# Scan ring of eight units, one C product for two units, two drive products in one instruction, and the state-space norm in the experts' tail

## What is computed

```python
h = _layernorm(x) * (1 + ca) + sa          # state-space norm
u, gate = split(h @ W_in.T)                # 1024 channels each
u = silu(causal_conv(u, 4 taps) + conv_b)
dt, B, C = split(u @ Wx.T); each _rmsnorm
delta = softplus(dt @ Wdt.T + dt_bias)
# scan over tokens t, for each of 1024 channels and 16 states
state = exp(delta_t * A) * state + (delta_t * u_t) * B_t
y_t = sum over states of state * C_t
x = x + ga * ((y + u * D) * silu(gate)) @ W_out.T
```

## Time and profile before

| | us |
|---|---|
| median of 3 runs | 1993.42 (1985.92 to 1998.05) |
| profiled execution, its own time | 1997.48 |
| its span, first to last instruction | 1995.7 |
| start of the state-space stage | 784.65 |
| first scan | 884.79 |
| end of the last scan | 1872.1 |

### The profile page before, as it was taken

How to read it: one execution, slowest core, us unless ns; L and a number is a source line. 1 busy time by engine, 2 the same in 40 slices (tenths; PEclk the granted TensorE clock), 3 DMA queues, 4 the chain that set the end, 5 groups by cost and what they waited for, 6 DMA issues and landing times. The chain is left out here.

```text
span 1995.7 us, 24404 instructions
## 1 busy us (share of the span) xinstructions
PE 1644.5 (82%) x8256; PEld 881.9 (44%) x8256; DVE 1394.3 (70%) x2276; ACT 1083.1 (54%) x1989; POOL 998.4 (50%) x590
## 2 busy tenths in 40 slices
PE   6888999999689994869689697896978969755758
PEld 2522232232256443747356474663746637422422
DVE  3258888886173112048999989899899898999523
ACT  2334666667511112265857668576685766754227
POOL 0000000001054004138898888888888888999413
PEclk8766999999855995869588696896978969766778
DMA  5311000000292436233443444434444344544122
GB/s 220 150 55 50 3 3 3 3 3 4 40 354 98 132 111 231 95 89 92 112 101 85 109 119 108 111 80 106 112 114 117 82 102 106 120 102 98 35 100 85
DMA packets 150747, 191.58 MB, mean 96 GB/s; under 512 B 17715, under 2 KB 122947, under 8 KB 148958
## 3 DMA queue, kind: packets, MB, share of 16 engines
q1 hardware_dynamic: 142508, 167.19, 30.9%
q0 software_dynamic: 4608, 16.80, 2.4%
q10 hardware_dynamic: 3508, 6.05, 0.8%
HBM read 141.81 MB, written 48.18 MB: 95 GB/s over the span
## 5 line engine op out<-in xcount | busy, mean ns | idle before, releaser
L1760 DVE TENSOR_TENSOR_SCAN ssm_scan<-ssm_psum,ssm_state,ssm_scan 128x256 f32<-128x256 f32 x1024 | 678.7, 728 | 49.8 <-ACT ssm_psum L1636 49.3
L1343 POOL TENSOR_TENSOR ssm_scan<-ssm_scan,ssm_bc 128x1024 f32<-128x1024 f32 x256 | 553.5, 2175 | 60.0 <-DVE ssm_scan L1760 58.8
L1636 ACT ACTIVATE ssm_psum<-ssm_rep,ssm_a 128x256 f32<-128x256 f32 x1024 | 433.4, 468 | 168.4 <-DVE ssm_scan L1760 167.9
L1467 PE MATMUL ssm_psum<-ssm_scan,ssm_select 128*32 128x256 f32 x2048 | 204.7, 481 | 199.3 <-POOL ssm_scan L1343 199.2
L1328 POOL TENSOR_TENSOR ssm_scan<-ssm_rep,ssm_bc 128x1024 f32<-128x1024 f32 x128 | 301.1, 2353 | 62.8 <-PE ssm_psum L1467 53.1
L640 ACT ACTIVATE att_probs<-att_psum 128x1024 f32<-128x1024 f32 x256 | 248.3, 1021 | 104.5 <-PE att_psum L576 104.2
L677 DVE TENSOR_REDUCE att_rowmax<-att_psum 128x1 f32<-128x512 f32 x448 | 277.9, 682 | 38.0 <-PE att_psum L558 38.0
L1467 PEld LDWEIGHTS ssm_psum<-ssm_scan,ssm_select 128*32 128x32 f32 x2048 | 45.8, 119 | 316.4 <-POOL ssm_scan L1343 216.4
L529 POOL COPY att_v<-v_tokens 128x128 f32<-128x128 f32 x8 | 2.3, 292 | 328.0 <-ACT att_out L634 328.0
L558 PE MATMUL att_psum<-att_k,att_q 72*128 72x512 bf16 x448 | 159.3, 395 | 3.7 <-DVE att_rowmax L677 2.2
L1745 DVE TENSOR_TENSOR ssm_scan<-ssm_rep,ssm_psum 128x1024 f32<-128x1024 f32 x128 | 155.5, 1215 | 8.5 <-PE ssm_psum L1467 5.8
(11 more groups left out here) (230 smaller groups left out, 1950.9 us busy)
## 6 DMA issues: line engine op xcount, KB each, us to landing
ssm_rep<-drive_rows SPq DMA_DIRECT2D x256, 256.0 KB, 4.4
qkv_wmod<-in_wmod SPq DMA_DIRECT2D x8, 1536.0 KB, 12.2
moe_we<-in_we SPq DMA_DIRECT2D x8, 1024.0 KB, 14.2
ssm_bc<-bc_rows SPq DMA_DIRECT2D x32, 256.0 KB, 4.9
drive_rows<-ssm_delta SPq DMA_DIRECT2D x64, 128.0 KB, 1.7
drive_rows<-ssm_du SPq DMA_DIRECT2D x64, 128.0 KB, 1.8
sorted_rows<-moe_zeros SPq DMA_DIRECT2D x1, 5888.0 KB, 19.1
moe_sorted<-sorted_rows SPq DMA_DIRECT2D x23, 256.0 KB, 3.5
```

Of the source, the lines that this page charges most:

```text
L1343: nc.gpsimd.tensor_tensor(read[:, Q % RING], drive[:, Q % RING], bc[:, c % 2, 1, gr, :].unsqueeze(1).to_broadcast([P, J, SW]), ALU.mult).t ...
L1467: last = nc.tensor.matmul(ps_y[t % 2][32 * j:32 * j + 32, :], select[:], read[:, Q % RING, j, :], start=(gr == 0), stop=False)
L1636: nc.scalar.activation(ps_decay[n % HALF_BANKS][:, i], rep[:, s % 2, 0, j, :], ACT.Exp, scale=amat[:, t, gr, j:j + 1]).then_inc(decay_done, 1)
L1760: nc.vector.tensor_tensor_scan(drive[:, Q % RING, j, :], ps_decay[(2 * Q + j // 2) % HALF_BANKS][:, j % 2], drive[:, Q % RING, j, :], stat ...
```

## The change

In `state_space`:

- the ring has 8 slots;
- GpSimd's drive products of units 0 and 2 of a channel tile are one instruction (`spread(s)`), issued for tile s+1 ahead of the C product of the second unit of tile s; it waits for the copy of tile s+1 in `rep` and for the sum of unit 4s-2;
- the C products of two units are one instruction, after the scans of the second; its semaphore rises by 2 when both are done;
- `drive_input` of tile t+2 stays behind the C product that holds the second unit of tile t;
- the norm of the chunk is gone; chunk data come in normalised, and ScalarE only modulates them, in place, in two buffers;
- the output product adds the residual by two products with the identity, W_out is multiplied with the layer's gate once by GpSimd, and ScalarE copies the result out (`copy_out`); VectorE's `residual` is gone; the gated y overwrites the gate;
- the tables change: "out" goes to units 10, 11, 12, 14, "gate" to 16, 17, 27, 28; ScalarE takes them away at 12, 13, 14, 16 and 18, 19, 29, 30, and the gate's SiLU is at 31;
- of chunk 0, two gate pieces and two step pieces are done in units 0 to 5 (`LATE`) and not ahead of the first scan.

In `experts`: the tail also normalises x (statistics, root, reciprocal, and the product by ScalarE for 12 tiles and by VectorE for 4), stores x with tokens on partitions and the normalised one turned. W_in and W_out lie in the room of the experts' weights, u in that of the turned tiles; half of W_in is loaded in the tail.

```diff
--- before.py
+++ after.py
...
-    RING = 4
+    RING = 8
...
-        AT = {0: ("proj", 0), 1: ("proj", 1), 3: ("conv", 0), 4: ("proj", 2), 5: ("conv", 1), 6: ("proj", 3), 7: ("conv", 2), 8: ("mean", 0),
-              9: ("conv", 3), 10: ("gate", 0), 11: ("gate", 1), 12: ("gate", 2), 13: ("rows", 0), 14: ("gate", 3), 15: ("square", 0),
-              16: ("out", 0), 17: ("out", 1), 18: ("var", 0), 19: ("rms", 0), 20: ("bcast", 0), 21: ("step", 0), 22: ("step", 1),
-              24: ("step", 2), 25: ("step", 3), 27: ("out", 2), 28: ("out", 3)}
-        AHEAD = {"proj": 1, "conv": 1, "gate": 1, "rows": 1, "square": 1, "rms": 1, "step": 1, "mean": 2, "var": 2, "bcast": 2, "out": -1}
-        FIRST = (("mean", 0, 0), ("var", 0, 0), ("bcast", 0, 0), ("proj", 0, 0), ("proj", 0, 1), ("conv", 0, 0), ("proj", 0, 2), ("conv", 0, 1),
-                 ("proj", 0, 3), ("conv", 0, 2), ("conv", 0, 3), ("gate", 0, 0), ("gate", 0, 1), ("rows", 0, 0), ("gate", 0, 2), ("square", 0, 0),
-                 ("gate", 0, 3), ("rms", 0, 0), ("step", 0, 0), ("step", 0, 1), ("step", 0, 2), ("step", 0, 3),
-                 ("mean", 1, 0), ("var", 1, 0), ("bcast", 1, 0))
+        AT = {0: ("proj", 0), 1: ("proj", 1), 3: ("conv", 0), 4: ("proj", 2), 5: ("conv", 1), 6: ("proj", 3), 7: ("conv", 2),
+              9: ("conv", 3), 10: ("out", 0), 11: ("out", 1), 12: ("out", 2), 13: ("rows", 0), 14: ("out", 3), 15: ("square", 0),
+              16: ("gate", 0), 17: ("gate", 1), 19: ("rms", 0), 21: ("step", 0), 22: ("step", 1),
+              24: ("step", 2), 25: ("step", 3), 27: ("gate", 2), 28: ("gate", 3)}
+        AHEAD = {"proj": 1, "conv": 1, "gate": 1, "rows": 1, "square": 1, "rms": 1, "step": 1, "out": -1}
+        FIRST = (("proj", 0, 0), ("proj", 0, 1), ("conv", 0, 0), ("proj", 0, 2), ("conv", 0, 1), ("proj", 0, 3), ("conv", 0, 2), ("conv", 0, 3),
+                 ("rows", 0, 0), ("square", 0, 0), ("rms", 0, 0), ("step", 0, 0), ("gate", 0, 0), ("gate", 0, 1), ("step", 0, 1))
+        LATE = {0: ("gate", 2), 1: ("step", 2), 2: ("gate", 3), 3: ("step", 3)}
...
-        U_COPY, CONV_OUT, GATE_OUT = {3: 0, 4: 1, 7: 2, 9: 3}, {6: 0, 8: 1, 10: 2, 12: 3}, {13: 0, 14: 1, 15: 2, 17: 3}
-        SILU, ROWS_OUT, RMS, SQUARE, GATE_SILU, RSTD, H_OUT = 13, 16, 18, 19, 20, 21, 24
+        U_COPY, CONV_OUT, GATE_OUT = {3: 0, 4: 1, 7: 2, 9: 3}, {6: 0, 8: 1, 10: 2, 12: 3}, {18: 0, 19: 1, 29: 2, 30: 3}
+        SILU, ROWS_OUT, RMS, GATE_SILU, H_OUT = 13, 16, 18, 31, 24
+        LATE_GATE, LATE_STEP, LATE_SILU, LATE_DELTA = {2: 2, 4: 3}, {3: 2, 5: 3}, 5, {3: 2, 5: 3}
         STEP_OUT = {24: 0, 25: 1, 27: 2, 28: 3}
         CARRY_HALO, SAVE_HALO = {1: 0, 2: 1, 6: 2, 8: 3}, {4: 0, 5: 1, 8: 2, 10: 3}
-        CENTRED, NORMED, NORM = 11, 21, 22
+        NORMED = 21
         DELTA = {24: 0, 25: 1, 27: 2, 28: 3}
-        RESIDUAL = {19: 0, 20: 1, 30: 2, 31: 3}
+        OUT_COPY = {12: 0, 13: 1, 14: 2, 16: 3}
...
-            def spread(Q):
-
-                c, q = Q // UNITS, Q % UNITS
-                t, gr = q // GROUPS, q % GROUPS
-                s = c * DT + t
+            def spread(s):
+
+                c, Q = s // DT, s * GROUPS
                 pool.wait_ge(rep_in[s % 2], 64 * (s // 2 + 1))
                 pool.wait_ge(bc_in[c % 2], 64 * (c // 2 + 1))
                 if Q >= RING:
-                    pool.wait_ge(sum_done, Q - RING + 1)
-                    pool.wait_ge(carry_done, (Q - RING) // 2 + 1)
-                nc.gpsimd.tensor_tensor(drive[:, Q % RING], rep[:, s % 2, 1],
-                                        bc[:, c % 2, 0, gr, :].unsqueeze(1).to_broadcast([P, J, SW]), ALU.mult).then_inc(pool_input, 1)
+                    pool.wait_ge(sum_done, Q + 2 - RING + 1)
+                    pool.wait_ge(carry_done, (Q + 2 - RING) // 2 + 1)
+                nc.gpsimd.tensor_tensor(drive[:, Q % RING:Q % RING + 3:2], rep[:, s % 2, 1].unsqueeze(1).to_broadcast([P, 2, J, SW]),
+                                        bc[:, c % 2, 0, 0::2, :].unsqueeze(2).to_broadcast([P, 2, J, SW]), ALU.mult).then_inc(pool_input, 2)
+
+            pool.wait_ge(g.win_in[2], 16)
+            pool.wait_ge(row_out, 1)
+            for t in range(DT):
+                nc.gpsimd.tensor_tensor(wout[:, t], wout[:, t], gate_row, ALU.mult).then_inc(wout_gated, 1)
 
             drive_input(0, 0)
             drive_input(0, 1)
-            for Q in range(2):
-                if not ON_DVE[Q]:
-                    spread(Q)
+            spread(0)
             for c in range(SCH):
                 for q in range(UNITS):
                     t, gr = q // GROUPS, q % GROUPS
                     Q = c * UNITS + q
-                    if Q + 2 < SCH * UNITS and not ON_DVE[(q + 2) % UNITS]:
-                        spread(Q + 2)
-                    pool.wait_ge(scan_done, (Q + 1) * J)
-                    nc.gpsimd.tensor_tensor(read[:, Q % RING], drive[:, Q % RING],
-                                            bc[:, c % 2, 1, gr, :].unsqueeze(1).to_broadcast([P, J, SW]), ALU.mult).then_inc(read_done, 1)
+                    if gr % 2:
+                        if gr == 1 and c * DT + t + 1 < SCH * DT:
+                            spread(c * DT + t + 1)
+                        pool.wait_ge(scan_done, (Q + 1) * J)
+                        pair = slice((Q - 1) % RING, Q % RING + 1)
+                        nc.gpsimd.tensor_tensor(read[:, pair], drive[:, pair],
+                                                bc[:, c % 2, 1, gr - 1:gr + 1, :].unsqueeze(2).to_broadcast([P, 2, J, SW]), ALU.mult).then_inc(read_done, 2)
                     c2, t2 = ahead(c, t)
...
             def output(c, m):
                 if m == 0:
                     pe.wait_ge(ygate_done, (c + 1) * DT)
+                    pe.wait_ge(wout_gated, DT)
                 for t in range(DT):
-                    last = nc.tensor.matmul(bank("out", c, m)[:, 0:SW], wout[:, t, m * P:(m + 1) * P], y[:, c % 2, t, :], start=(t == 0), stop=(t == DT - 1))
+                    nc.tensor.matmul(bank("out", c, m)[:, 0:SW], wout[:, t, m * P:(m + 1) * P], gate[:, c % 2, t, :], start=(t == 0), stop=False)
+                if m == 0:
+                    pe.wait_ge(xres_in, 16 * (c + 1))
+                for s in range(ST):
+                    last = nc.tensor.matmul(bank("out", c, m)[:, s * P:(s + 1) * P], xres[:, s, m * P:(m + 1) * P], g.ident[:], start=False, stop=(s == ST - 1))
...
             def modulate(c):
-                act.wait_ge(norm_done, c + 1)
+                act.wait_ge(x_in[c % 2], 16 * (c // 2 + 1))
                 for k in range(KT):
-                    last = nc.scalar.activation(h[:, k, :], x[:, k, :], ACT.Identity, bias=shift[:, k:k + 1], scale=scale[:, k:k + 1])
+                    last = nc.scalar.activation(h[:, c % 2, k, :], h[:, c % 2, k, :], ACT.Identity, bias=shift[:, k:k + 1], scale=scale[:, k:k + 1])
                 last.then_inc(h_done, 1)
...
+            def copy_out(c, m):
+                act.wait_ge(out_mm, c * KT + m + 1)
+                if m == 0:
+                    act.wait_ge(wout_gated, DT)
+                    if c >= 1:
+                        act.wait_ge(x3_stored, 16 * c)
+                nc.scalar.copy(xout[:, m, :], bank("out", c, m)[:, 0:SW]).then_inc(x3_done, 1)
...
-                if c >= 2:
-                    dve.wait_ge(out_mm, (c - 1) * KT)
-                nc.vector.tensor_tensor(y[:, c % 2, t, :], ps_y[t % 2], gate[:, c % 2, t, :], ALU.mult).then_inc(ygate_done, 1)
-
-            def residual(c, m):
-                if m == 0:
-                    dve.wait_ge(xres_in, 16 * (c + 1))
-                dve.wait_ge(out_mm, c * KT + m + 1)
-                nc.vector.scalar_tensor_tensor(xres[:, m, :], bank("out", c, m)[:, 0:SW], gates[:, m:m + 1], xres[:, m, :],
-                                               ALU.mult, ALU.add).then_inc(x3_done, 1)
...
+            for i in range(SCH):
+                sp.wait_ge(x2_done, (i + 1) * TC)
+                sp.dma_start(xdst[:, i * TC:(i + 1) * TC], x[:, i * TC:(i + 1) * TC]).then_inc(x2_stored, 16)
+                sp.wait_ge(hn_out, (i + 1) * TC)
+                sp.dma_start(hdst[:, :, i * SW:(i + 1) * SW], hnt[:, i % TSLOTS]).then_inc(g.hn_stored[i % TSLOTS], 16)
...
+            act.wait_ge(y_mm, TILES)
+            wsrc = d["win"].rearrange("(k p) m -> p k m", p=P)
+            act.dma_start(win[:, :, 0:DI], wsrc[:, :, 0:DI]).then_inc(g.win_in[0], 16)
...
+            for n in range(TT + 2):
+                if 0 <= n - 2 < TT:
+                    inverse2(n - 2)
+                if n < TT:
+                    add(n)
+                if 0 <= n - 1 < TT:
+                    variance2(n - 1)
+                if 0 <= n - 2 < TT:
+                    normalise2(n - 2)
+                if n < TT:
+                    statistics2(n)
```

320 lines of the change are left out of this document (158 added, 162 removed).

## The result

The changed kernel takes 2362.76 us (median of 4 runs, 2351.13 to 2366.03) against 1994.38 for the kernel before (4 runs, 1985.92 to 1998.05). The ratio is 1.185 with a 95% interval of 1.178 to 1.191: it is slower by over 18%. The forecast was 2292 with a range of 2100 to 2372. The profiled execution took 2366.03, its span is 2364.2.

What follows compares the result with a forecast made beforehand. No engine is full; waits between engines bound the scans, with TensorE without a gap in units 1 to 18. Span 1995.7 + 323 (scans) - 29 (ahead) + 5 (behind) = 2294.7, so 2292 us; range 2100 to 2372.

Steps and rivals of the forecast that it cites:

- the forecast's own run: Whole kernel: 166 a chunk and within some 6 of it, running from 2240 to 2350; chance 0.69.
- the slowest rival: Whole kernel: everything at TensorE's lower clock level and GpSimd products of 4.7, some 2371; chance beyond it 0.05.
- Later sums: TensorE and ScalarE: even units' sums wait for both units' C product, delaying pieces and decays; most of 323 us more.
- The walk: A middle chunk followed unit by unit, each start the latest of its predecessors: 171, or 160 with pieces at 3.65.
- the copy's ring: GpSimd and SyncE: copy 8.4, drive product, C product, delta·u close a ring of 17.7 per tile; alone 2107, chance 0.2.
- 166 for a middle chunk: Scans of chunks 1 to 6: 166 taken for each, with 171 and 160 from the unit-by-unit walk; together 996.
- Chunk 0: First chunk's scans: no output pieces (10 less), late gate and step pieces 14 more; 170.
- The last chunk: Only output pieces: six tiles at 17.7, two at 13.8, 10 for the copies at 12 to 16; 144.
- Two-unit results: ScalarE's output and gate pieces: ahead of an odd unit, two units later costs VectorE 6, three units later 3.3.
- The products: GpSimd's 128x2048 products: C 4.10, drive 4.46, pairing saving at most 48 us; by the skill's figure 38 us more.
- VectorE's lighter chunk: VectorE loses 4.3 per chunk of passes and residuals; not on the path, counted as nothing, 34 us if the bound.
- Ahead of the first scan: Start of the state-space stage: first scan at 855.5 to 856 against 884.79, a gain of 29.

Runs made afterwards that it cites:

- e3: Changed kernel with only delta·u of tile t+2 issued ahead of the drive product and the C product; 2319.8 us, 170.7 per chunk.
- e8: Changed kernel with 14 more filler products on TensorE ahead of the first sum of each channel tile from the second on; 2339.1 us, 171.8 per chunk.
- e10: Changed kernel with both pairings undone, output and gate results taken three units later, gate's SiLU moved behind unit 2's decays; 1944.2 us, 0.977 of the kernel before.
- e2: Changed kernel with only the next tile's drive product issued behind the first pair's C product and delta·u; 2305.6 us, 170.8 per chunk.
- e7: Changed kernel with C and drive products both made for one unit again and the scan ring back at four units; 2037.6 us, 132.8 per chunk.
- e5: Changed kernel with only the tables changed, output and gate pieces taken away three units later instead of two; 2269.3 us, 160.5 per chunk.

## Why the prediction was right, and where its steps were off

The side and the mechanism held: the pairs make TensorE's sums late, its pieces with them, and ScalarE and VectorE wait for the pieces in their queues. The size held less well. 2292 is 71 too low, and 2362.76 lies above the forecast's own run of 2240 to 2350. It is inside the stated range only because that was stretched to the slowest rival, 2371, which counted products of 4.7 where 4.16 was measured; that part is luck. Of the signs named in advance, GpSimd's waits for the copy (131), the scans' waits for decays (327), the C product (4.16) and the clock (0.77) came as said; the chunk (174.8, not 160 to 171) and the first scan (863.3, not 856) did not.

- **Later sums.** The walk can be laid beside the trace, tile by tile (means of chunks 1 to 6, from first scan to first scan):

| channel tile | 1 | 2 | 3 | 4 | 5 | 6 | 7 | 8 | chunk |
|---|---|---|---|---|---|---|---|---|---|
| walk, lower clock behind idle time | 18.5 | 18.1 | 24.7 | 26.1 | 21.6 | 20.7 | 18.8 | 22.5 | 171 |
| changed kernel | 19.5 | 20.9 | 24.7 | 26.5 | 21.3 | 21.0 | 19.2 | 21.6 | 174.8 |
| e3, delta·u first | 19.5 | 16.7 | 24.9 | 26.0 | 21.6 | 21.0 | 18.5 | 22.4 | 170.7 |

All but the second are within 1.0. The second is 2.8 too short in the walk, and e3 says why: it opens the copy's ring alone, and the second tile falls by 4.2. The wait for the copy in the timeline above (4.94 ahead of the drive product at 1415.54) is one of these. A wait that I had not counted also shows there: VectorE's carry of the halo, the tokens that the convolution needs from before (L1760), waits 34.5 us for the convolution in six waits of chunks 1 to 6, 7.69 in the timeline above. ScalarE waits for the same piece, and the scans behind it wait 0.30 more for their decays, so by itself it costs little.
- **166 for a middle chunk is the step that failed in size.** Measured were 174.8; the six chunks together took 1048.5 and not 996, which is 52.5 of the 71. Of the 8.8 per chunk, 5 were lost when I took the middle between the walk's 171, with the clock that the rows show behind an idle stretch, and its 160 with every piece at the upper level. There was no reason to shade the walk towards the upper level, since it had itself produced the idle time that comes before the lower one, and the trace has it: behind 4.74 of idle time a piece takes 6.30, and the clock is 0.77. The 11 us between the two walks were never measured; e8 gives 3 as a lower bound. The other 3.8 are mostly the copy in the second tile.
- **Chunk 0**: 170 forecast, 178.9 measured. Its first two tiles take 25.6 and 25.9. In e10, without pairs, they take 20.0 and 20.1 and those of chunk 1 take 15.0 and 13.7, so the late gate and step pieces cost 11 by themselves and the pairing comes on top.
- **The last chunk**: 144 forecast, 142.6 measured. The copy's ring is worth 17.6 of it, as e3 shows, but the sum agrees better than its parts: it was six tiles at 17.7 and 10 for the output pieces, and the tiles took 14.2, 14.9, 31.0, 18.3, 13.3, 14.6, 19.7 and 16.8.
- **The copy's ring** was put at 17.7 per tile. In the last chunk the drive products start 18.5 to 20.0 apart; from delta·u's end to the drive product pass 9.2 to 10.4 and not 8.4. The 8.4 took the median landing time, 4.3, for the last of the four parts; the last one lands latest, 5.5 after its issue, which makes 9.6 in the trace before and a ring of 18.9. As the only cause (2107) it is refuted. "Ring slots don't help, since it is the read-back that is late" was wrong in the middle chunks: there 28 of 48 drive products wait for TensorE's sum, which frees the ring's slots, and 20 for the read-back (the view below has 29 and 19, since it names a sum for the one at 1415.54). It mattered little: e2 takes nearly all of both waits away for 4 us per chunk, and e7 shows the ring's length to be worth 0.8 without pairs.

What the drive product waited for from 1039 to 2087 in the changed kernel (us, times), and GpSimd's timeline in its last chunk (delta·u, drive product, twice):

```profile
  PE ssm_psum L1531: 114.4, 29
  DMA ssm_rep<-drive_rows: 81.9, 19
```

```profile
2162.33 0.73 POOL L1397 TENSOR_TENSOR ssm_du<-ssm_delta,late_turned 128x256 f32<-128x256 f32 x1
...
2172.32 4.51 POOL L1407 TENSOR_TENSOR ssm_scan<-ssm_rep,ssm_bc 128x2048 f32<-128x2048 f32 x1 [2.27 <-DMA ssm_rep<-drive_rows]
...
2180.91 0.73 POOL L1397 TENSOR_TENSOR ssm_du<-ssm_delta,late_turned 128x256 f32<-128x256 f32 x1
...
2191.99 4.50 POOL L1407 TENSOR_TENSOR ssm_scan<-ssm_rep,ssm_bc 128x2048 f32<-128x2048 f32 x1 [6.23 <-DMA ssm_rep<-drive_rows]
```

- **Two-unit results**: 2.7 at each of eight pieces would be 21.6 per chunk, measured 14.3 (e5). Not every piece was on the path.
- **The products**: C 4.16 and drive 4.52, forecast 4.10 and 4.46. The Trainium skill's 4497 ns (GPSIMD Engine Reference, 3.1, Elementwise) is for an add of two inputs; it agrees with the drive product within 1%, and the C product is 8% below it. The forecast's estimate from that figure was too small: three instructions of 4.497 and delta·u make 14.22 per channel tile, an estimate of 0.8 more than 13.39 and 53 us over 64 tiles, not 0.6 and 38. The 38 us of the slowest rival also counts one of a tile's two C products at 4.7. GpSimd's work per channel tile comes to 13.57 (forecast 13.39), and as it waits for the scans either way, the difference decided nothing.
- **VectorE's lighter chunk**, counted at nothing, is nothing here. Once the waits are gone, e10's chunk is 3.9 shorter than before, as VectorE's busy time is (110.7 against 114.5).
- **Ahead of the first scan** the forecast was 856, measured 863.30, a gain of 21.5 and not 29. The stage begins at 789.00 instead of 784.65, and the modulation starts 7.0 after it and not 4.7. Behind the last scan 7.3 are added, not 5.

SyncE's and ScalarE's first rows of the stage, for the last point:

```profile
789.00 0.36 SPq L1306 DMA_DIRECT2D ssm_h<-x_layer_normalised  x1
```

```profile
796.00 2.08 ACT L1586 ACTIVATE ssm_h<-ssm_h,mod 128x256 f32<-128x256 f32 x4 [5.22 <-DMA ssm_h<-x_layer_normalised]
```

52.5 of the middle chunks, 8.9 of chunk 0, 7.3 and 2.3 at the ends, less 1.4 of the last chunk, are the 70 between forecast and span. What stays open: how the 27 to 36 us per chunk of the pairing of C split between the even unit's wait for the odd unit's scans, the longer product, and two pieces in a row on TensorE. No run separates these.

## What to carry to other kernels

Merging two instructions to save a fixed cost of a fifth of a microsecond is dear where a consumer was working on the first half: the first result then comes as late as the second, and every queue behind it, tied by fixed orders, is late too. Look for the engine that has threaded other work between the two halves, and ask what the distance between giving and taking a result covers after the merge. A table-loading function belongs where its engine already waits, which the idle time in a timeline row shows; one such move was worth 5 us per chunk here. Where a read-back is issued in parts, count the landing of the last part and not the median. And where a row names who ended a wait for several semaphores, check that this one was needed.

## What the runs showed of the hardware

GpSimd's 128x2048 products took 4.16 us (C) and 4.52 us (drive), twice the 2.176 and 2.354 of the half size less 0.19: a larger product saves that much and no more. Of the four parts of a read-back, issued within 1.35 us, the last landed 5.9 us after its issue where the median of the four was 4.7. Fourteen added products per channel tile raised the granted clock from 0.77 to 0.90, and a chunk got 3.0 us of 174.8 shorter, though the products themselves delayed most sums; a rise from 0.85 to 0.90 came with no gain, under the same flaw. The start of a stage whose preceding code was the same in all thirteen kernels lay between 774.6 and 794.0; I did not find out why.
